# An attention and mixture-of-experts kernel on one core: the second norm's and the router's chained VectorE steps get a tick each

## The chip, the cores and the metric

The kernel runs on one core of one Trainium2 chip. The metric is the device time in microseconds (us) of one execution, the median of three runs. Engines are named PE (TensorE; PEld is its weight load), DVE (VectorE), ACT (ScalarE), POOL (GpSimd) and SP (SyncE, which here only issues DMAs; SPq, POOLq and so on are their queues).

## What is computed

`x` has 8 batches of 512 tokens with 128 channels, all float32.

```
x = x + attention(layernorm(x))          # 16 heads of 8 channels, causal, softmax over 512 keys
x = x + experts(layernorm(x))
# experts: logits = x_n @ Wg (8 experts), the top two of 8 by jax.lax.top_k, gates = softmax of the two logits * alpha
# each token's two experts: layernorm -> fc1 (128 to 512) -> gelu -> fc2 (512 to 128), summed with the gates
```

## The kernel before

**Order of the work.** One list, `schedule`, is built at the start, and every engine walks it and carries out those of its entries that concern it, in that order. The list is ordered by ticks. There are 352 units of attention work, 11 for each of 32 groups of four heads, 44 for each batch; a unit is a bank of scores: one head of 512 columns, one of 384, two of 256 or four of 128. In tick n PE makes the scores of unit n for the row maximum (`pass1`, L644 and L648), then those of unit n-24 again, shifted by the maximum (`pass2`, L665), and, in four of eleven ticks, a row of probabilities times values (`pv`, L680). DVE takes the row maximum of unit n (L940 for one head, L934 for several), ACT the exponential of unit n-24 (L811) and POOL cuts that one's diagonal (L1252). The tables `FRONT`, `APPLY`, `SPLIT`, `FIRST_HALF`, `SECOND_HALF`, `GROUP`, `BACK` and `ROUTE` (L36 to L47) then put all other steps behind the units of given ticks. `FRONT` counts from the start of the batch before, `ROUTE` and `BACK` from the start of their own; since the pattern repeats every 44 ticks, a step at 109 of one batch stands at tick 21 of a period, and this text gives ticks in the period, 0 to 43, in brackets where they matter.

**The score banks.** Both passes share a ring of six banks (`slots`), so PE may begin `pass1` of unit n only when DVE has done the maximum of unit n-3: PE runs at most three ticks ahead of DVE.

**The bank `misc`.** All other PE results go through one bank, in the order maxT [6], xnT [8], q [10], the attention's output projection [13], k [15], maxT [17], zT [24], gate [26], maxT [28], v [31], rank [36], maxT [39]. PE claims it (`claim`) only when the result before it has been read (semaphore `s_free`). A reader (DVE or ACT) takes a result at the start of the next tick, or ahead of the next use of the bank if that stands in the same tick. xnT, q, k, v and zT are read by ACT (L769, L778, L823), the others by DVE.

**First norm of the next batch.** DVE `ln_stats` [1] and `aggregate` [3] (mean and variance, then `var_eps`), POOL `rsqrt` [3] (L1163), DVE `ln_apply` four times [6] (L893), then PE xnT, q and k. POOL's `split` makes the bf16 parts of q and k, SP lays them out by DMA (`stack`).

**The batch's second norm and router.** DVE `r_stats` [14], `r_agg` [17], POOL `rsqrt_two` [17] (L1184), DVE `make_z` [21] (four rows L893 and `ratio` L976), PE zT [24] (L602), gate [26] (L707), ACT `copy_z` [26], DVE `top_two` [30] (L987 to L1005), POOL `second_gate` [31] (L1191), DVE `combine` [34] (L1010 to L1020), PE `rank` [36] (L715 to L721), whose reader on DVE, `put_places` (L1026 to L1034), runs ahead of the maximum of tick 37. POOL then sends the 512 tokens with their two copies off with eight indirect DMAs, `dispatch` (L1235), three ticks apart from [35] on; the first waits for `combine` and `put_places`. Within `top_two`, `combine`, `put_places` and the two `agg` steps, an instruction that reads the one before it waits for its end: `link` lets it raise `s_ln` and makes DVE wait for that count at once. There are 15 such links in a batch.

**The last ticks.** `SOONER` moves the steps of batch 6 forward; what of batch 7 lies behind tick 383 is placed by `LATE` between the expert tiles. Batches 0 to 5 are dispatched by tick 364; the table of the first 17 expert tiles is made in ticks 359 to 363 and loading starts at tick 366. Behind the attention come 39 tiles of expert work (L731 to L756).

## Time and profile before

| | |
|---|---|
| median of 3 runs | 540.84 us (540.76 to 541.0) |
| profiled execution, span | 560.3 us |
| busy: PE, DVE, POOL, ACT | 85%, 67%, 65%, 58% of the span |
| a period of 44 ticks with a router in it, steady | 43.09 us |
| granted TensorE clock there | 1.00 |

The profiled execution has no time of its own beside its span; that is 19.5 us above the median. Times below are microseconds from the start of this span. Busy time of short instructions overlaps: the distance of two starts says what one costs.

### The profile page before, as it was taken

How to read it: one execution, taken by the hardware profiler on the slowest of the kernel's cores; microseconds unless marked ns; L12 is line 12 of the kernel's file. 1: busy time of each engine (PE TensorE's matmuls, PEld its weight loads, DVE VectorE, ACT ScalarE, POOL GpSimd, SP SyncE). 2: the span in 40 equal slices, each digit the busy share in tenths (PEclk: the TensorE clock that was granted, in tenths of full speed). 3: DMA queues.
4: the chain of work that ended last, by engine and by line, in shares of the span. 5: the costliest groups of instructions: out<-in, count | busy, mean ns of one | idle time of the engine just before them, and what ended most of it. 6: DMA issues, size and time to landing. Idle time of an engine off the chain costs nothing.

```text
span 560.3 us, 11807 instructions
## 1 busy us (share of the span) xinstructions
PE 473.9 (85%) x3296; PEld 277.1 (49%) x3296; DVE 373.1 (67%) x1316; ACT 322.9 (58%) x661; POOL 366.1 (65%) x712
## 2 busy tenths in 40 slices
PE   3379999999999998998898988786992999999930
PEld 1134443543443453443444443364981888888920
DVE  4588878889889889889889997741543521222226
ACT  2137786776676776676676666752550555565610
POOL 5956676586986986987887876955556444445520
PEclk9589999999999999999999999897996899999985
DMA  2323133134233234234224212276642685666439
GB/s 62 93 57 105 65 93 109 58 105 118 68 101 117 78 87 129 73 91 130 75 66 130 71 40 79 79 236 213 219 159 86 213 264 180 216 194 187 154 129 328
DMA packets 52726, 70.83 MB, mean 126 GB/s; under 512 B 11063, under 2 KB 38430, under 8 KB 52662
## 3 DMA queue, kind: packets, MB, share of 16 engines
q1 hardware_dynamic: 47478, 59.19, 34.7%
q0 software_dynamic: 4320, 8.53, 4.5%
q10 hardware_dynamic: 864, 2.36, 1.2%
q8 instruction: 27, 0.44, 0.3%
q14 instruction: 37, 0.30, 0.2%
HBM read 36.49 MB, written 20.94 MB: 102 GB/s over the span
## 4 chain that ended last, share of the span: by engine, by line
PE 51%; DVE 17%; issue 8%; POOL 6%; SPq 5%; DMA 4%; another core or an unknown queue 4%; ACT 3%; ACTq 0%; DVEq 0%; POOLq 0%
PE acc_bank L748 10%; PE slots L739 10%; PE slots L648 7%; PE acc_bank L680 7%; PE slots L665 5%; SPq L496 4%; DVE masked L940 3%; PE misc L616 3%; POOL z_dram L1235 2%; DVE z L893 2%; DVE row_max L934 2%; POOL probs L1252 2%; DMA y_in<-y_dram 2%; PE slots L644 2%
## 5 line engine op out<-in xcount | busy, mean ns | idle before, releaser
L811 ACT ACTIVATE probs<-slots 128x512 f32<-128x512 f32 (+1 forms) x352 | 185.6, 562 | 86.0 <-PE slots L665 79.2
L940 DVE CUSTOM_DVE_ANT_0 masked<-slots,causal_row 128x512 bf16<-128x512 f32 (+1 forms) x256 | 148.9, 614 | 20.8 <-PE slots L648 20.7
L648 PE MATMUL slots<-stack_k,stack_q 125*128 125x256 bf16 (+3 forms) x512 | 128.5, 307 | 19.4 <-DVE row_max L940 7.5
L1252 POOL TENSOR_SCALAR_AFFINE_SELECT probs<-probs 128x128 f32<-128x128 f32 (+2 forms) x352 | 116.1, 350 | 41.3 <-ACT probs L811 37.4
L665 PE MATMUL slots<-stack_q,stack_k 128*128 128x256 bf16 (+3 forms) x512 | 125.6, 301 | 2.9 <-DVE row_max L934 1.5
L1282 POOL DMA_INDIRECT y_dram<-y,z_in x71 | 69.7, 982 | 73.4 <-DVE y L1126 56.8
L841 ACT ACTIVATE hidden<-slots,w_in 128x256 f32<-128x256 f32 (+1 forms) x156 | 63.1, 455 | 82.6 <-PE acc_bank L748 29.2
L680 PE MATMUL acc_bank<-probs,v 128*32 128x512 f32 (+3 forms) x1024 | 95.6, 447 | 3.4 <-POOL probs L1252 2.7
L648 PEld LDWEIGHTS slots<-stack_k,stack_q 125*128 125x128 bf16 x512 | 48.3, 99 | 95.4 <-DVE row_max L940 49.7
L1235 POOL DMA_INDIRECT z_dram<-z,pos x64 | 63.6, 994 | 32.1 <-DVE pos L1034 17.7
L748 PE MATMUL acc_bank<-hidden,w_in 128*128 128x256 f32 (+1 forms) x312 | 73.0, 376 | 7.8 <-issue 4.0
L934 DVE TENSOR_REDUCE row_max<-slots 128x2 f32<-128x512 f32 (+1 forms) x96 | 63.7, 689 | 14.0 <-PE slots L648 13.2
L739 PE MATMUL slots<-hdnT,w_in 128*128 128x256 f32 (+1 forms) x312 | 71.1, 372 | 1.4 <-ACT hdnT L834 0.7
L748 PEld LDWEIGHTS acc_bank<-hidden,w_in 128*128 128x128 f32 x312 | 54.6, 196 | 15.9 <-ACT hidden L841 5.8
L739 PEld LDWEIGHTS slots<-hdnT,w_in 128*128 128x128 f32 x312 | 57.4, 197 | 9.8 <-issue 1.9
L665 PEld LDWEIGHTS slots<-stack_q,stack_k 128*128 128x128 bf16 x512 | 46.0, 98 | 25.7 <-issue 6.5
L1126 DVE TENSOR_TENSOR y<-slots,z_in 128x256 f32<-128x256 f32 (+1 forms) x39 | 15.6, 400 | 54.4 <-issue 33.5
L1120 DVE TENSOR_SCALAR yT<-acc_bank,w_in 128x256 f32<-128x256 f32 (+1 forms) x39 | 17.8, 457 | 49.8 <-PE acc_bank L748 37.4
L680 PEld LDWEIGHTS acc_bank<-probs,v 128*32 128x32 f32 x1024 | 20.4, 108 | 36.9 <-issue 17.2
L644 PE MATMUL slots<-causal,ident_b 128*128 128x256 bf16 (+1 forms) x96 | 30.6, 319 | 0.2 <-DVE row_max L940 0.2
L834 ACT ACTIVATE hdnT<-slots,w_in 128x256 f32<-128x256 f32 (+1 forms) x39 | 21.2, 543 | 2.8 <-PE slots L731 2.8
L756 PE MATMUL slots<-ident,yT 128*128 128x128 f32 x71 | 14.6, 280 | 8.0 <-issue 7.6
(168 smaller groups left out, 523.1 us busy)
## 6 DMA issues: line engine op xcount, KB each, us to landing
w_in<-in_wpack SPq DMA_DIRECT2D x39, 516.0 KB
o_dram<-oT SPq DMA_DIRECT2D x32, 256.0 KB, 2.3
stack_k<-parts SPq DMA_DIRECT2D x95, 64.0 KB
stack_q<-parts SPq DMA_DIRECT2D x93, 64.0 KB
z_in<-z_dram SPq DMA_DIRECT2D x32, 132.0 KB
xt<-in_x SPq DMA_DIRECT2D x8, 256.0 KB, 3.7
onT<-o_dram SPq DMA_DIRECT2D x8, 256.0 KB
o_inv<-inv_dram SPq DMA_DIRECT2D x8, 256.0 KB
```

Source lines behind the costliest of these rows:

```text
L648: mm = pe.matmul(cols[:, i, :], q[0:K1, hh, blk * P:blk * P + P], k[0:K1, hh, 0:w], start=len(heads) == 1, stop=True, skip_group_check=True)
L665: mm = pe.matmul(cols[:, i, :], k[0:K2, hh, blk * P:blk * P + P], q[0:K2, hh, blk * P:T], start=True, stop=True)
L680: mm = pe.matmul(acc_bank[32 * h:32 * h + 32, row * P:T], v1[:, b % 2, row, HPG * hg + h, :], p, start=(row == 0), stop=(row == PV_ORDER[- ...
L739: pe.matmul(half(slots[:, k, :], i), weights(i)[:, k * P:k * P + P], hdnT[:, i % 2, 0:rows_of(i)], start=True, stop=True)\
L748: mm = pe.matmul(half(acc_bank[:, :], i), weights(i)[:, F + k * C:F + k * C + C], hidden[:, i % 2, k, 0:rows_of(i)], start=k == 0, stop=k ...
L811: act.activation(probs_of(n), columns(n, slot), ACT.Exp, scale=SCALE).then_inc(s_exp, 1)
L841: act.activation(hidden[:, i % 2, k, 0:rows_of(i)], half(slots[:, k, :], i), ACT.Gelu_apprx_tanh, bias=aux(i, 2 + k))\
L934: dve.tensor_reduce(largest, columns(n, slot), AX.X, ALU.max).then_inc(s_max, 1)
L940: dve.tensor_tensor_reduce(out=masked[:, n % MASKED, 0:w], in0=slots[:, slot, 0:w], in1=causal_row[:, T - w:T], scale=1.0, scalar=NEG, op0 ...
L1235: pool.indirect_dma_start(out=z_dram[:, :], out_offset=bass.IndirectOffsetOnAxis(ap=pos[:, b % 2, i:i + 1], axis=0), in_=z[:, b % 2, j, n, ...
L1252: pool.affine_select(out=diag, in_=diag, compare_op=ALU.is_ge, fill=0.0, base=0, pattern=[[0, len(heads)], [1, P]], channel_multiplier=-1) ...
L1282: pool.indirect_dma_start(out=y_dram[:, :], out_offset=bass.IndirectOffsetOnAxis(ap=z_in[:, i % Z_RING, n, ID:ID + 1].bitcast(U32), axis=0 ...
```

## The change

The steps of the second norm and of the router of batches 0 to 5 are cut up: each instruction (or pair) that another waits for becomes an entry of its own in the tick table. `link` becomes `step` (raise the count) and `stepped` (wait for it, ahead of the next step). The same instructions are issued; the row `base` gets a second copy, so that its update no longer waits for its reader. The new ticks in the period, for batches 0 to 5: stats [14, 15], aggregate [16], variances and POOL's root [17], the four rows of z [23, 24, 25, 26], zT [27], copy [29], gate [30], maximum [31], index [32], difference [33], scaled and POOL's `second_gate` [34], pick [35], select [36], rank [37], sum [38], first gate and mask of places [39], second gate and sum of places [40], alpha and store of places [41], store of gates and the first dispatch [42]. Batch 5's dispatches lie two ticks apart instead of three. Batches 6 and 7 keep their order. The first norm of batches 1 to 7: aggregate [2], variance and POOL's root [3], rows [7, 8, 8, 9], xnT [10], q [12], k [17], and the splits and stacks up to two ticks later. In tick 17, k stands ahead of maxT.

```diff
--- before.py
+++ after.py
@@ -33,21 +33,29 @@
 PV_LAG = 7
 
 
-FRONT = {"ln_stats": 1, "ln_agg": 3, "xnT": 8, "q": 10, "k": 15, "v": 31}
-APPLY = (6, 6, 6, 6)
-SPLIT = ((11, 12, 16, 18), (17, 18, 26, 29))
-FIRST_HALF = ((15, 20, 22), (19, 28, 31))
-SECOND_HALF = ((29, 30, 31), (32, 33, 34))
+FRONT = {"ln_stats": 1, "ln_agg": 2, "ln_var": 3, "xnT": 10, "q": 12, "k": 17, "v": 31}
+APPLY = (7, 8, 8, 9)
+SPLIT = ((13, 14, 18, 20), (19, 20, 28, 31))
+FIRST_HALF = ((17, 22, 24), (21, 30, 33))
+SECOND_HALF = ((29, 30, 31), (34, 35, 36))
 GROUP = {"max_parts": 11, "maxT": 17}
 BACK = {"residual": 40, "o_load": 45, "o_invert": 56, "o_spread": 61, "o_scale": 65,
         "proj": 68}
-ROUTE = (("r_stats", 102), ("r_agg", 105), ("r_root", 105), ("r_z", 109), ("zT", 112), ("gate", 114), ("r_top", 118),
-         ("r_exp", 119), ("r_copy", 114), ("r_comb", 122), ("rank", 124))
-DISPATCH, DISPATCH_STEP = 123, 3
+ROUTE = (("r_stats", 102, 0), ("r_stats", 103, 1), ("r_agg", 104), ("r_var", 105), ("r_root", 105),
+         ("r_z", 111, 0), ("r_z", 112, 1), ("r_z", 113, 2), ("r_z", 114, 3), ("zT", 115), ("gate", 118), ("r_copy", 117),
+         ("r_max", 119), ("r_index", 120), ("r_diff", 121), ("r_scaled", 122), ("r_exp", 122), ("r_pick", 123),
+         ("r_sel", 124), ("rank", 125), ("g_sum", 126), ("g_first", 127), ("g_second", 128), ("p_mask", 127),
+         ("g_alpha", 129), ("p_sum", 128), ("g_store", 130), ("p_store", 129))
+STEPS_OF = {"r_stats": (("r_stats", 0), ("r_stats", 1)), "r_agg": (("r_agg",), ("r_var",)),
+            "r_z": tuple(("r_z", n) for n in range(4)),
+            "r_top": (("r_max",), ("r_index",), ("r_diff",), ("r_scaled",), ("r_pick",), ("r_sel",)),
+            "r_comb": (("g_sum",), ("g_first",), ("g_second",), ("g_alpha",), ("g_store",)),
+            "places": (("p_mask",), ("p_sum",), ("p_store",))}
+LAST_ROUTE = (("r_stats", 94), ("r_agg", 95), ("r_root", 97), ("r_z", 101), ("zT", 109), ("gate", 111), ("r_copy", 111),
+              ("r_top", 115), ("r_exp", 116), ("r_comb", 116), ("rank", 118), ("places", 119))
+DISPATCH, DISPATCH_STEP, LAST_EARLY_STEP = 130, 3, 2
 BY_SCALAR = (("stack", 0, 0, 1, 0), ("stack", 0, 0, 2, 0), ("stack", 0, 1, 2, 0))
-SOONER = {(6, "o_invert"): 8, (6, "o_spread"): 8, (6, "o_scale"): 8, (6, "proj"): 8, (6, "r_stats"): 8,
-          (6, "r_agg"): 10, (6, "r_root"): 8, (6, "r_z"): 8, (6, "zT"): 3, (6, "gate"): 3,
-          (6, "r_top"): 3, (6, "r_exp"): 3, (6, "r_copy"): 3, (6, "r_comb"): 6, (6, "rank"): 6}
+SOONER = {(6, "o_invert"): 8, (6, "o_spread"): 8, (6, "o_scale"): 8, (6, "proj"): 8}
...
     for b in range(B):
         n = NG * UNITS * b
-        for name, m in ROUTE:
-            at(n + m - SOONER.get((b, name), 0), name, b)
+        if b < EARLY_BATCHES:
+            for name, m, *part in ROUTE:
+                at(n + m, name, b, *part)
+        else:
+            for name, m in LAST_ROUTE:
+                for step, *part in STEPS_OF.get(name, ((name,),)):
+                    at(n + m, step, b, *part)
         for i in range(2 * NT):
-            at(n + DISPATCH + DISPATCH_STEP * i - SOONER.get((b, "dispatch"), 0), "dispatch", b, i)
+            step = LAST_EARLY_STEP if b == EARLY_BATCHES - 1 else DISPATCH_STEP
+            at(n + DISPATCH + step * i, "dispatch", b, i)
         if b == EARLY_BATCHES - 1:
             for i, step in enumerate(TABLE):
...
+            def step(ins):
+
+                ins.then_inc(s_ln, 1)
+                chain[0] += 1
+
+            def stepped():
+
+                dve.wait_ge(s_ln, chain[0])
+
...
-            def mean_variance():
+            def mean_variance(*_):
                 dve.wait_ge(s_stats, stats_no[0])
                 for n in range(NT):
                     last = dve.bn_aggr(mean_var[:, n, :], stats[:, n, :])
-                link(last)
-
-            def aggregate(*_):
-                mean_variance()
+                step(last)
+
+            def add_eps(*_):
+                stepped()
                 dve.tensor_scalar(var_eps[:, :], mean_var[:, :, 1], EPS, None, ALU.add).then_inc(s_var, 1)
                 variance_no[0] += 1
 
...
-            def make_z(b):
-                wait(dve, s_rtwo, b + 1)
-                wait(dve, s_disp[b % 2], 16 * 2 * NT * (b // 2))
-                normalise(z[:, b % 2, 0, :, 0:C], xt[:, NT * b:NT * b + NT, :], rstd_two[:, 0, :]).then_inc(s_z, 1)
-                dve.tensor_tensor(ratio[:, :], var_two[:, 0, :], rstd_two[:, 0, :], ALU.mult).then_inc(s_ratio, 1)
+            def make_z(b, n):
+                if n == 0:
+                    wait(dve, s_rtwo, b + 1)
+                    wait(dve, s_disp[b % 2], 16 * 2 * NT * (b // 2))
+                ins = normalise(z[:, b % 2, 0, :, 0:C], xt[:, NT * b:NT * b + NT, :], rstd_two[:, 0, :], (n,))
+                if n == NT - 1:
+                    ins.then_inc(s_z, 1)
...
-            def top_two(b):
+            def find_max(b):
 
                 wait(dve, s_free, misc_no[("gate", b)] + 1)
                 for n in range(NT):
                     last = dve.max(top[:, n, :], gate_in[:, n, :])
-                link(last)
+                step(last)
+
+            def find_index(b):
+                stepped()
                 for n in range(NT):
                     last = dve.max_index(top_at[:, n, :], top[:, n, :], gate_in[:, n, :])
-                link(last)
+                step(last)
+
+            def difference(b):
+                wait(dve, s_second, b)
+                dve.wait_ge(s_ratio, b + 1)
+                stepped()
+                dve.tensor_tensor(denom[:, :], ratio[:, :], rstd_two[:, 1, :], ALU.mult)
+                step(dve.tensor_tensor(diff[:, :], top[:, :, 1], top[:, :, 0], ALU.subtract))
+
...
+            def gate_sum(b):
                 wait(dve, s_second, b + 1)
-                link(dve.tensor_scalar(denom[:, :], second[:, :], 1.0, None, ALU.add))
-                link(dve.reciprocal(gates[:, 0, :], denom[:, :]))
-                link(dve.tensor_tensor(gates[:, 1, :], gates[:, 0, :], second[:, :], ALU.mult))
+                step(dve.tensor_scalar(denom[:, :], second[:, :], 1.0, None, ALU.add))
+
+            def gate_first(b):
+                stepped()
+                step(dve.reciprocal(gates[:, 0, :], denom[:, :]))
+
...
-            def put_places(b):
+            def find_places(b):
                 wait_filled(dve, ("rank", b))
                 if b == 0:
-                    link(dve.tensor_copy(base[:, :], region[:, :]))
-                link(dve.tensor_tensor(place_of[:, :, :], misc[:, 0:NT * E].rearrange("p (n e) -> p n e", e=E),
-                                       base[:, :].rearrange("p (a e) -> p a e", a=1).broadcast_to([P, NT, E]), ALU.add))
-                dve.tensor_tensor(base[:, :], misc[:, NT * E:NT * E + E], base[:, :], ALU.add).then_inc(s_free, 1)
-                link(dve.tensor_tensor(by_place[:, :, :, :].rearrange("p j n e -> p j (n e)"),
+                    link(dve.tensor_copy(base[:, 0, :], region[:, :]))
+                step(dve.tensor_tensor(place_of[:, :, :], misc[:, 0:NT * E].rearrange("p (n e) -> p n e", e=E),
+                                       base[:, b % 2:b % 2 + 1, :].broadcast_to([P, NT, E]), ALU.add))
+                dve.tensor_tensor(base[:, (b + 1) % 2, :], misc[:, NT * E:NT * E + E], base[:, b % 2, :], ALU.add)                   .then_inc(s_free, 1)
+
+            def mask_places(b):
+                stepped()
+                step(dve.tensor_tensor(by_place[:, :, :, :].rearrange("p j n e -> p j (n e)"),
...
```

The other steps (`scaled`, `pick_two`, `select`, `gate_second`, `gate_alpha`, `gate_store`, `sum_places`, `store_places`) are cut out of the old functions in the same way.

## Rows read from the trace of the kernel before

**Rows 1.** The page: busy us, share of the span and instructions.

```profile
PE 473.9 (85%) x3296; PEld 277.1 (49%) x3296; DVE 373.1 (67%) x1316; ACT 322.9 (58%) x661; POOL 366.1 (65%) x712
```

**Rows 2.** Windows: us, busy (count) of PE, PEld, DVE, ACT, POOL, granted clock, DMA.

```profile
60.45:97.37 36.92, 36.13 (x290) 16.03 (x288) 29.44 (x95) 28.16 (x57) 24.34 (x68) 1.00 0.30 90
184.20:227.29 43.09, 39.76 (x322) 18.03 (x316) 38.47 (x142) 30.07 (x59) 34.98 (x76) 1.00 0.33 96
```

**Rows 3.** Waits in 199.17:242.26, one period: us, times, longest us.

```profile
PEld slots L648 <- DVE row_max L940: 6.9, 10, 1.2
...
POOL z_dram L1235 <- DVE pos L1034: 2.5, 1, 2.5
...
PEld acc_bank L680 <- POOL probs L1252: 1.5, 5, 0.4
...
PE misc L602 <- DVE max_rows L948: 1.0, 1, 1.0
...
DVE xn L893 <- POOL rstd L1163: 0.9, 1, 0.9
```

**Rows 4.** Timeline of DVE inside one router: start us, us.

```profile
213.27 0.22 DVE L1015 TENSOR_TENSOR by_alpha<-pick,alpha_s 128x64 f32<-128x64 f32 x1
213.53 0.22 DVE L1018 TENSOR_REDUCE alpha_of<-by_alpha 128x8 f32<-128x64 f32 x1
213.78 0.17 DVE L1019 COPY z<-token_ids 128x8 int32<-128x8 int32 x1
213.86 0.17 DVE L1020 TENSOR_TENSOR z<-alpha_of,gates 128x8 f32<-128x8 f32 x1
```

**Rows 5.** Timelines of DVE and POOL, and DVE's groups by line (busy, mean ns).

```profile
208.72 0.54 DVE L996 TENSOR_TENSOR denom<-ratio,rstd_two 128x4 f32<-128x4 f32 x1
...
207.97 1.27 POOL L1276 TENSOR_TENSOR xt<-xt,bp_s 128x512 f32<-128x512 f32 x1
...
L893 DVE TENSOR_SCALAR z<-xt,mean_var,rstd_two 128x128 f32<-128x128 f32 x32 | 14.9, 525 | 1.2 <-POOL rstd_two L1184 1.2
...
L893 DVE TENSOR_SCALAR xn<-xt,mean_var,rstd 128x128 f32<-128x128 f32 x32 | 9.1, 344 | 5.1 <-POOL rstd L1163 5.1
```

**Rows 6.** Timeline of PE and ACT around results in `misc`.

```profile
235.37 1.13 PE L616 MATMUL misc<-xnT,wqkv_s 128*128 128x512 f32 x2
236.33 0.33 PE L648 MATMUL slots<-stack_k,stack_q 125*128 125x384 bf16 x1
236.53 0.69 ACT L778 ACTIVATE qk<-misc,bqk_s 128x512 f32<-128x512 f32 x1 [0.39 <-PE misc L616]
...
201.03 0.63 PE L602 MATMUL misc<-ident,z 128*128 128x128 f32 x4 [0.22 <-DVE z L893]
...
201.69 0.60 ACT L769 ACTIVATE zT<-misc 128x512 f32<-128x512 f32 x1 [0.25 <-PE misc L602]
```

**Rows 7.** Timeline of POOL behind the router.

```profile
216.43 1.05 POOL L1235 DMA_INDIRECT z_dram<-z,pos  x1 [2.52 <-DVE pos L1034]
...
226.15 1.04 POOL L1163 TENSOR_TENSOR rstd<-var_eps,minus_half 128x4 f32<-128x4 f32 x1
```

**Rows 8.** Timeline of PE: gate, rank, and the unit held up behind it.

```profile
202.83 0.95 PE L707 MATMUL misc<-wg_s,zT 128*128 128x8 f32 x8
203.64 0.32 PE L648 MATMUL slots<-stack_k,stack_q 125*128 125x384 bf16 x1
...
213.19 0.18 PE L715 MATMUL misc<-sel,tri_b 128*128 128x32 bf16 x1
...
213.40 0.32 PE L648 MATMUL slots<-stack_k,stack_q 125*128 125x384 bf16 x1
...
214.69 0.34 PE L648 MATMUL slots<-stack_k,stack_q 125*128 125x384 bf16 x1 [0.75 <-DVE row_max L940]
```

**Rows 9.** Timeline of PE at the attention's end.

```profile
354.23 1.06 PE L680 MATMUL acc_bank<-probs,v 128*32 128x512 f32 x8 [0.89 <-POOL probs L1252]
...
359.28 0.64 PE L680 MATMUL acc_bank<-probs,v 128*32 128x256 f32 x8 [1.80 <-POOL probs L1252]
```

73 lines of the change are left out of this document (45 added, 28 removed).

## The prediction

> **What bounds the kernel now.** I began with the page's busy shares: PE 473.9 of 560.3 us, DVE 373.1, POOL 366.1 [rows 1]. No engine is full on the whole, so the stage has to be looked at. The change moves nothing but steps of the attention, which repeats every 44 ticks; so the next view was the windows of one such period. Two of them are a measurement in themselves: from the rows of the first norm to the next such rows it is 36.92 us where no router runs and 43.09 us where one does [rows 2]. A router thus costs 6.2 us a batch, six times. In its period PE is busy 39.8 us, DVE 38.5, POOL 35.0: three engines at 81 to 92%, none of them full, tied by the ring of six banks. Then the waits of that period [rows 3]: the largest of PE is for a row maximum of DVE, 6.9 us over 10 times; POOL waits once, 2.5 us, for the router's places; PE waits 1.0 us at xnT, and DVE 0.9 us for the first norm's root. The timelines say why. Within a router DVE does eleven small instructions between two maxima, and PE, at most three ticks ahead, runs dry: 0.75 us at 214.69 [rows 8]. In other stretches (228 to 241) PE has hardly a gap. So the pace changes hands, and this decides the sum: a microsecond saved on DVE counts where DVE leads, one added on PE counts where PE leads.
>
> **The parts of the change, for one period.** The number of instructions stays the same; what changes is waiting and place.
>
> *Links.* Of 15 links 12 get a maximum between the two instructions, and the waits are then met when they come up. Three stay: the mask of places stands right behind the first gate, and the sum and the store of places right behind a step of the gates, and each waits for the instruction ahead of it. Price: linked instructions of the router start 0.26 and 0.25 us apart, two without a link 0.08 [rows 4]. The unlinked one is itself 0.05 shorter (0.17 against 0.22), so I take 0.12 a link; the ends are 0 (if a small instruction between two maxima costs more than one in a row) and 0.17. 12 x 0.12 = 1.4 us off DVE, nearly all in the stretch that DVE leads: **-1.4**, ends -2.0 and 0.
>
> The Trainium skill speaks against this term: "VectorE: DVE Perf Modes", section "The DRAIN you can't avoid", says a semaphore behind every instruction costs a chain of copies nothing, and advises to save instructions and not semaphores. By it the term would be 0; the rows above show otherwise.
>
> *The bunch.* Beyond the links, spreading puts 0.1 to 0.6 us behind each maximum in place of 2.4 us behind one, so the ring of three ticks covers it. PE's dry spells behind the router are 0.75 us [rows 8], and much of that is the links again; I take **-0.4**, ends -0.8 and 0.
>
> *First norm's rows.* They come four ticks behind their variance instead of three, and POOL is less behind, so DVE's 0.9 us for the root [rows 3] goes. What is late next is PE's xnT: the last row is at tick 9, xnT at 10, and PE again waits for DVE, as it did for 1.0 us [rows 3]. **-0.3**, ends -0.9 and +0.4.
>
> *Second norm's rows.* A row of z takes 525 ns on average where the same instruction for the first norm takes 344 [rows 5]; `denom` took 0.54 us and ended with a POOL instruction that had started before it (207.97 + 1.27 = 209.24, 208.72 + 0.54 = 209.26) [rows 5]. So DVE is held up by POOL at these. At 23 to 26 the rows stand clear of the two splits in tick 20 in part. Of 4 x 0.18 and some 0.4 of the small ones I take half: **-0.5**, ends -1.0 and 0.
>
> *First dispatch.* POOL arrives at 213.91 and waits 2.52 us [rows 7], diagonals of later units behind it, and is then without a gap until the root at 226.15 [rows 7]. Now places and gates are due at ticks 41 and 42 and the dispatch at 42. POOL arrived about one maximum ahead of DVE, so I expect 0.7 us of wait. PE waited for cuts 1.5 us in this period [rows 3]: **-0.6**, ends -1.5 and 0.
>
> *The bank `misc`.* This is the cost side; each new neighbour makes PE wait for a reader. (a) k and maxT share tick 17: PE could go on at 236.33, ACT has read k by 236.53 + 0.6 = 237.1 [rows 6]; +0.8. (b) q at 12, projection at 13: the same read, less the 0.45 us of tick 13's matmuls; +0.35. Both lie in the stretch that PE leads: **+1.15**. (c) zT 27, maxT 28: ACT's copy begins 0.25 behind the transposes' last (201.69) and takes 0.6 [rows 6], less 0.3 of matmuls; +0.45. (d) gate 30, v 31: v waits until DVE, up to three ticks behind, has read the gate; PE is dry for the bank, then DVE for the 0.8 to 0.9 us of v; +0.5, ends 0 and 1.0. Both lie where DVE leads, and I count half: **+0.5**. (e) select 36, rank 37: PE waits for DVE, but DVE has the maximum of 37 (0.6 us) to do meanwhile, and a rank takes 0.21 [rows 8]: 0, with an upper end of +0.7.
>
> *The queues.* SP issues the same DMAs, the last stack two ticks later (36 in place of 34), eight ticks before the next batch's first unit, so 0. POOL's `second_gate` waits for DVE's scaled difference of its own tick, cover: the sum that uses it is four ticks later, so 0; without the cover it would be a POOL instruction of 1 us on DVE's path.
>
> *Sum.* -1.4 - 0.4 - 0.3 - 0.5 - 0.6 + 1.15 + 0.5 = -1.55 us a period; times 6, -9.3. In periods without a router only the first norm's changes count, and there PE leads (36.13 of 36.92 busy [rows 2]): +0.8 for k and +0.35 for q less 0.3, about +0.9 once. At the end of the attention PE waits for POOL's cuts (0.89 and 1.80 us [rows 9]); batch 5's dispatches, packed into ticks 350 to 364, are seven instead of five behind tick 352, but POOL has not lost its 2.5 us ahead of them: 0, ends -1 and +2. Batches 6 and 7 and the expert tiles keep their order: 0. Total -8.4.
>
> The sum is made on the profiled execution: 560.3 to 551.9 us. That one is 19.5 us longer than the median of 540.84; the attention is not where such time would go by anything the trace shows, so I carry the difference over unscaled: 540.84 - 8.4 = **532.5 us**.
>
> **The rivals.**
>
> *A. PE alone sets the pace.* If spreading hides all of the router's DVE work, a period is the one without router plus PE's own work for it: 36.92 + gate 0.81 + rank 0.21 [rows 8] + projection, like the gate, 0.85 + zT 0.4 + 0.8 for k = 40.0 us. That is 3.1 x 6 = 18.6 less, and 0.9 more for the front: **523 us**. For it: DVE was 29.4 of 36.92 busy without a router [rows 2], so there is room. Against it: the router adds 9.0 us to DVE and 10.6 to POOL. Chance 0.15.
>
> *B. Slower: the bank `misc`.* If DVE's savings fall where PE leads or is held by `misc`, what remains is the links (-1.4) against all of the bank's waits (0.8 + 0.35 + 0.45 + 0.5): +0.7 a period, 4.2 in six, and +0.9 for the front: 5 us, **546 us**. It decides from the point where PE's new waits pass DVE's savings, 2.1 against 1.4. For it: 228 to 241 is PE's; k, q and xnT are in it. Against it: PE's 6.9 us of waits for maxima show DVE leading elsewhere. Chance 0.20.
>
> *C. No change.* If the links are free, since a small instruction by itself between two large ones costs about what it did, the sum is -0.15 a period, 0.9 in six, against +0.9 for the front: **541 us**. This would also be the time if POOL set the pace. Chance 0.10.
>
> The DRAIN rule of the Trainium skill's "VectorE: DVE Perf Modes" is this case; the unlinked start 0.08 us behind speaks against it.
>
> **How the numbers follow.** The forecast has 0.55, A 0.15, B 0.20, C 0.10. A measurement of this kernel can tell 0.2%, 1.1 us, from no change. Faster 0.70, same 0.10, slower 0.20. The range leaves out the outer half of A (0.07) and of B (0.10): 523 to 546 us.
>
> **What the changed profile would show.** Links: between two maxima one or two small DVE instructions, none 0.25 behind another but the three named. Bunch: the wait of PE for L940 below 5 us a period. POOL's wait ahead of its first dispatch below 1 us. First norm: DVE's wait for the root gone, PE's wait at xnT still there. Bank: gaps of 0.8 us on PE between k and maxT and 0.3 to 0.5 at the projection and at the maxT behind zT. A period of 41.5 us instead of 43.09. The prediction is wrong if the period stays above 42.8 or falls under 40.3, or if the expert part changes by over 2 us.

## The result, and the profile of the changed kernel

The changed kernel is slower: 557.43 us (median of four runs) against 540.92 for the kernel before on the same chip, ratio 1.030 [1.028, 1.032]. The prediction said 532.5.

The two profiled executions can't be compared as wholes. In that of the kernel before (560.3 us) ACT stood idle for 23.4 us in the expert part, for something the trace calls "remote"; in that of the changed kernel (554.1 us) it did not. On one of the chips used below the kernel before takes 541 us again, and the four traces taken there (e9 to e12) show no such waits; on the others it takes 562 to 565 us, and every trace taken there shows 12 to 25 us of them for ACT in the expert part. From batch 2 on the attention of the changed kernel has none, and its periods repeated within 0.05 us on another chip (e5).

So the attention is measured by a landmark that both kernels have 352 times, once in each tick: the start of DVE's row maximum. From that of tick 5 to that of tick 5 of the next batch it takes, in us:

| batch | 0 | 1 | 2 | 3 | 4 | 5 | 6 | last maximum at |
|---|---|---|---|---|---|---|---|---|
| before | 32.98 | 36.92 | 42.27 | 43.62 | 43.10 | 43.08 | 41.63 | 345.0 |
| changed | 33.42 | 39.28 | 44.77 | 45.56 | 45.38 | 45.37 | 44.25 | 358.7 |

A period is 2.28 us longer instead of 1.55 shorter, and batch 1, which has no router in it yet, is 2.36 longer. The last maximum comes 13.7 us later. What follows it is longer too: 217.7 us in e5 against 215.3 in the kernel before, both with "remote" waits, and 1.5 of these 2.4 us lie ahead of PE's last product with v, where the prediction had 0. The windows of batch 4, cut at the maxima of the ticks 5, 12, 19, 24, 27, 31, 37, 43 and 5, show where (us, then busy us and count of PE, PEld, DVE, ACT, POOL, the granted clock, DMA share, GB/s). First the kernel before:

```profile
182.31:189.06 6.75, 5.67 (x52) 3.09 (x55) 5.87 (x20) 4.24 (x9) 6.16 (x13) 1.00 0.29 101
189.06:196.65 7.59, 7.59 (x52) 3.02 (x51) 6.11 (x29) 6.05 (x12) 6.86 (x16) 1.00 0.19 55
196.65:202.30 5.65, 5.26 (x44) 2.48 (x43) 5.39 (x11) 4.13 (x8) 5.42 (x12) 1.00 0.37 110
202.30:204.10 1.80, 1.80 (x13) 1.21 (x12) 1.80 (x9) 1.63 (x4) 1.61 (x5) 1.00 0.57 159
204.10:210.02 5.92, 5.92 (x56) 3.17 (x55) 4.53 (x27) 4.32 (x10) 4.02 (x8) 1.00 0.20 51
210.02:216.08 6.06, 4.65 (x39) 1.57 (x39) 5.79 (x23) 3.58 (x7) 3.19 (x9) 1.00 0.41 123
216.08:219.88 3.80, 3.71 (x37) 1.80 (x36) 3.49 (x13) 1.98 (x5) 3.24 (x7) 1.00 0.55 138
219.88:225.41 5.53, 5.13 (x37) 1.68 (x34) 5.50 (x23) 4.11 (x8) 4.50 (x12) 1.00 0.31 97
```

The same stretches of the changed kernel:

```profile
188.65:195.13 6.48, 5.40 (x55) 2.99 (x56) 5.86 (x20) 3.87 (x8) 6.06 (x13) 1.00 0.37 114
195.13:204.81 9.68, 8.56 (x53) 3.29 (x47) 6.33 (x29) 6.11 (x12) 8.72 (x17) 1.00 0.15 45
204.81:209.91 5.10, 4.92 (x41) 2.34 (x41) 4.84 (x9) 4.31 (x10) 4.57 (x8) 1.00 0.42 123
209.91:212.54 2.63, 1.34 (x10) 0.27 (x10) 2.63 (x12) 1.27 (x3) 2.33 (x8) 1.00 0.42 117
212.54:217.48 4.94, 4.52 (x42) 2.73 (x42) 2.79 (x10) 2.89 (x6) 2.89 (x8) 1.00 0.13 34
217.48:223.23 5.75, 4.91 (x37) 2.67 (x37) 5.18 (x28) 4.68 (x9) 4.37 (x10) 1.00 0.43 133
223.23:229.00 5.77, 5.49 (x56) 2.55 (x57) 5.00 (x25) 2.90 (x6) 2.56 (x9) 1.00 0.41 113
229.00:234.03 5.03, 4.33 (x33) 1.28 (x31) 5.03 (x24) 3.79 (x8) 3.70 (x10) 1.00 0.27 86
sum 45.38, PE 39.47 PEld 18.10 DVE 37.65 ACT 29.81 POOL 35.20; mean PE 4.93 PEld 2.26 DVE 4.71 ACT 3.73 POOL 4.40
```

Neither of the two hot engines has more to do in the sum: DVE 37.65 us against 38.47, PE 39.47 against 39.73 (with 327 records for 330, so PE's difference may be one of recording). Yet PE stands idle for 5.9 us instead of 3.4. The largest loss is in the second row: before, PE was full there (7.59 of 7.59); now the same seven ticks take 9.68, of which PE works 8.56. The ticks 37 to 43 lose nearly as much (5.77 for 3.80), but the ten ticks ahead of them gain 1.3 (10.69 for 11.98). In the rows from 209.91 to 217.48 the two engines take turns: DVE 2.63 of 2.63 with PE at 1.34, then PE 4.52 of 4.94 with DVE at 2.79. The ring holds three ticks and does not bridge that.

The waits of one period of the changed kernel (190.91 to 236.29; us, times, longest), which answer to [rows 3]:

```profile
PEld slots L663 <- DVE row_max L964: 6.8, 8, 1.3
...
DVE masked L964 <- PE slots L663: 2.5, 3, 1.5
POOL z_dram L1300 <- issue: 2.4, 8, 0.8
DVE row_max L958 <- PE slots L663: 2.2, 5, 0.6
...
PE misc L617 <- DVE xn L917: 1.0, 1, 1.0
DVE xt L988 <- PE misc L710: 1.0, 1, 1.0
PE misc L730 <- DVE sel L1047: 1.0, 1, 1.0
...
DVE gate_in L1007 <- PE misc L722: 0.8, 1, 0.8
PE misc L702 <- ACT qk L793: 0.8, 1, 0.8
...
DVE xn L917 <- POOL rstd L1228: 0.6, 1, 0.6
```

POOL's 2.5 us for the places are gone. What is new stands beside `misc` and on DVE: rank waits for select, the gate's copy for the gate, the maxima's transpose for ACT's reading of k. PE's wait for the maxima is what it was, 6.8 against 6.9. In the timeline of PE and ACT (start, us, in brackets the idle time ahead):

```profile
197.14 0.69 ACT L793 ACTIVATE qk<-misc,bqk_s 128x512 f32<-128x512 f32 x1 [1.36 <-PE misc L631]
197.88 1.16 PE L710 MATMUL misc<-wp_s,onT 128*128 128x128 f32 x8 [0.34 <-ACT qk L793]
...
203.10 0.24 PE L702 MATMUL misc<-ident_b,max_parts 128*48 128x128 bf16 x1 [0.78 <-ACT qk L793]
...
223.45 0.18 PE L730 MATMUL misc<-sel,tri_b 128*128 128x32 bf16 x1 [1.01 <-DVE sel L1047]
```

The two waits for ACT that the prediction priced at 0.35 and 0.8 are there with 0.34 and 0.78. And DVE beside POOL at the first of z's rows:

```profile
207.61 1.17 POOL L1309 TENSOR_TENSOR parts<-qk,parts 128x512 bf16<-128x512 f32 x1
208.19 1.79 DVE L917 TENSOR_SCALAR z<-xt,mean_var,rstd_two 128x128 f32<-128x128 f32 x1
208.73 1.16 POOL L1309 TENSOR_TENSOR qk<-qk,parts 128x512 f32<-128x512 f32 x1
210.51 0.34 DVE L917 TENSOR_SCALAR z<-xt,mean_var,rstd_two 128x128 f32<-128x128 f32 x1
```

A row takes 0.34 us by itself; the one that began inside POOL's split took 1.79 and ended 0.09 behind the second split. The splits had moved two ticks with the first norm's part, and so had followed the rows that were moved away from them.

### The profile page after: what moved, and what is told of

It reads as the page before. It is cut to its first block, busy times and chain, and to the rows that moved or that the text cites. A ratio compares the mean times of both kernels' runs of the same rounds, so it can differ in the third digit from the quotient of the medians.

```text
span 554.1 us, 11776 instructions
## 1 busy us (share of the span) xinstructions
PE 467.1 (84%) x3264; PEld 274.2 (49%) x3296; DVE 366.4 (66%) x1316; ACT 321.2 (58%) x661; POOL 369.0 (67%) x712
## 3 DMA queue, kind: packets, MB, share of 16 engines
q10 hardware_dynamic: 864, 2.36, 1.2%
## 4 chain that ended last, share of the span: by engine, by line
PE 54%; DVE 16%; issue 11%; POOL 6%; DMA 5%; SPq 3%; ACT 3%; ACTq 0%; DVEq 0%; POOLq 0%
PE slots L754 11%; PE acc_bank L763 10%; PE acc_bank L695 8%; PE slots L663 7%; PE slots L680 5%; DVE masked L964 4%; DVE row_max L958 3%; PE misc L631 3%; SPq L511 2%; POOL probs L1317 2%; DMA y_in<-y_dram 2%; PE misc L617 2%; POOL z_dram L1300 2%; DVE xn L917 2%; ACT qk L793 2%
## 5 line engine op out<-in xcount | busy, mean ns | idle before, releaser
L826 ACT ACTIVATE probs<-slots 128x512 f32<-128x512 f32 (+1 forms) x352 | 182.4, 562 | 92.3 <-PE slots L680 83.2
L964 DVE CUSTOM_DVE_ANT_0 masked<-slots,causal_row 128x512 bf16<-128x512 f32 (+1 forms) x256 | 152.3, 614 | 26.9 <-PE slots L663 25.9
L1317 POOL TENSOR_SCALAR_AFFINE_SELECT probs<-probs 128x128 f32<-128x128 f32 (+2 forms) x352 | 119.0, 352 | 66.1 <-ACT probs L826 61.5
L680 PE MATMUL slots<-stack_q,stack_k 128*128 128x384 bf16 (+3 forms) x507 | 124.4, 301 | 2.9 <-DMA stack_q<-max_rows 2.5
L763 PE MATMUL acc_bank<-hidden,w_in 128*128 128x256 f32 (+1 forms) x312 | 68.1, 361 | 0.0
L754 PEld LDWEIGHTS slots<-hdnT,w_in 128*128 128x128 f32 x312 | 56.2, 193 | 9.1 <-issue 1.9
L680 PEld LDWEIGHTS slots<-stack_q,stack_k 128*128 128x128 bf16 x512 | 45.8, 98 | 28.8 <-issue 8.3
L763 PEld LDWEIGHTS acc_bank<-hidden,w_in 128*128 128x128 f32 x312 | 53.0, 190 | 5.0
L1188 DVE TENSOR_TENSOR y<-slots,z_in 128x256 f32<-128x256 f32 (+1 forms) x39 | 15.6, 400 | 45.8 <-PE slots L771 45.8
L964 DVE DVE_READ_ACCUMULATOR2_ANT row_max<- 128x1 f32 x256 | 21.0, 82 | 0.0
L659 PE MATMUL slots<-causal,ident_b 128*128 128x256 bf16 (+1 forms) x69 | 20.3, 294 | 0.4 <-DVE row_max L964 0.2
```

What stands on the lines that cost most here:

```text
L680: mm = pe.matmul(cols[:, i, :], k[0:K2, hh, blk * P:blk * P + P], q[0:K2, hh, blk * P:T], start=True, stop=True)
L754: pe.matmul(half(slots[:, k, :], i), weights(i)[:, k * P:k * P + P], hdnT[:, i % 2, 0:rows_of(i)], start=True, stop=True)\
L763: mm = pe.matmul(half(acc_bank[:, :], i), weights(i)[:, F + k * C:F + k * C + C], hidden[:, i % 2, k, 0:rows_of(i)], start=k == 0, stop=k ...
L826: act.activation(probs_of(n), columns(n, slot), ACT.Exp, scale=SCALE).then_inc(s_exp, 1)
L964: dve.tensor_tensor_reduce(out=masked[:, n % MASKED, 0:w], in0=slots[:, slot, 0:w], in1=causal_row[:, T - w:T], scale=1.0, scalar=NEG, op0 ...
L1317: pool.affine_select(out=diag, in_=diag, compare_op=ALU.is_ge, fill=0.0, base=0, pattern=[[0, len(heads)], [1, P]], channel_multiplier=-1) ...
```

## The experiments

All of them keep the changed kernel's code and move steps among ticks; the diffs of the tables are shortened to the entries that change. The table gives stretches of one period, measured as above and taken from batches in which the granted clock was 1.00 (batch 4, or the batch named), then the periods of batches 3, 4 and 5 as they came, and the ratio to the kernel before on the same chip. e12 has no row, since the clock fell in each of its batches from 3 on.

| run | 5-12 | 12-19 | 19-27 | 27-37 | 37-43 | 43-5 | periods | ratio |
|---|---|---|---|---|---|---|---|---|
| before | 6.75 | 7.59 | 7.45 | 11.98 | 3.80 | 5.53 | 43.6 43.1 43.1 | |
| changed | 6.48 | 9.68 | 7.73 | 10.69 | 5.77 | 5.03 | 45.6 45.4 45.4 | 1.030, e5 1.028 |
| e1 | 7.61 | 7.58 | 7.46 | 11.21 | 4.32 | 5.24 | 43.8 43.4 43.4 | 1.008 [1.005, 1.012] |
| e2 | 7.10 | 9.68 | 8.05 | 11.83 | 4.33 | 5.03 | 49.4 46.0 46.0 | 1.036 [1.032, 1.039] |
| e3 | 7.92 | 7.59 | 6.77 | 12.08 | 4.13 | 5.23 | 45.4 43.7 43.8 | 1.009 [1.007, 1.011] |
| e4 (batch 3) | 7.26 | 7.59 | 8.67 | 9.59 | 5.77 | 5.23 | 44.1 46.8 45.3 | 1.017 [1.010, 1.024] |
| e6 | 7.11 | 9.07 | 8.04 | 11.84 | 4.33 | 5.03 | 45.8 45.4 45.4 | 1.026 [1.019, 1.032] |
| e7 | 6.04 | 7.59 | 8.64 | 9.60 | 5.51 | 5.31 | 45.7 42.7 45.7 | 1.005 [1.000, 1.009] |
| e8 | 6.93 | 7.58 | 8.67 | 11.22 | 4.32 | 5.24 | 44.3 44.0 46.7 | 1.015 [1.008, 1.022] |
| e9 | 6.48 | 9.68 | 7.72 | 10.33 | 5.77 | 5.03 | 45.2 45.0 45.0 | 1.029 [1.028, 1.031] |
| e10 (batch 6) | 7.76 | 7.68 | 8.77 | 10.69 | 5.77 | | 52.6 49.8 51.3 | 1.052 [1.049, 1.054] |
| e11 (batch 5) | 6.69 | 7.69 | 8.07 | 10.42 | 5.52 | 5.29 | 43.9 44.8 43.7 | 1.015 [1.013, 1.018] |
| e13 | 6.25 | 9.67 | 6.86 | 11.16 | 5.80 | 5.03 | 44.4 44.8 44.7 | 1.024 [1.020, 1.029] |
| e14 (batch 5) | 6.40 | 7.59 | 7.54 | 10.03 | 7.11 | 5.35 | 44.8 45.4 44.0 | 1.017 [1.013, 1.021] |
| e15 (batch 3) | 5.89 | 7.58 | 7.55 | 9.60 | 5.55 | 5.30 | 41.5 42.0 41.5 | 1.005 [1.003, 1.008] |
| e16 | 5.98 | 9.76 | 6.86 | 10.68 | 5.99 | 5.12 | 44.2 44.4 44.6 | 1.036 [1.033, 1.039] |
| e17 | 5.96 | 7.58 | 7.59 | 9.59 | 5.58 | 5.30 | 41.5 41.6 42.6 | 0.999 [0.997, 1.001] |
| e18 | 5.99 | 7.58 | 7.59 | 9.58 | 5.37 | 5.51 | 42.4 41.6 42.3 | 0.995 [0.993, 0.997] |

### The three parts alone (e1 to e4)

**e1**: all steps back at their old ticks; only the steps of the places come one maximum later.

```diff
-FRONT = {"ln_stats": 1, "ln_agg": 2, "ln_var": 3, "xnT": 10, "q": 12, "k": 17, "v": 31}
-APPLY = (7, 8, 8, 9)
...
-DISPATCH, DISPATCH_STEP, LAST_EARLY_STEP = 130, 3, 2
+FRONT = {"ln_stats": 1, "ln_agg": 3, "ln_var": 3, "xnT": 8, "q": 10, "k": 15, "v": 31}
+APPLY = (6, 6, 6, 6)
...
+         ("r_z", 109, 0), ("r_z", 109, 1), ("r_z", 109, 2), ("r_z", 109, 3), ("zT", 112), ("gate", 114), ("r_copy", 114),
...
+DISPATCH, DISPATCH_STEP, LAST_EARLY_STEP = 123, 3, 3
```

> The changed code with every step put back to its old tick (cut-up steps of one group share a tick, so each waits for the one ahead of it as under the old links; the steps behind the place of a token run one maximum later than before). Theory (ticks decide, the code that cuts them up costs nothing): within 0.5% of the kernel before, 538 to 543.5 us. Rival (more entries and semaphore counts cost by themselves): 545 us or more.

Period 43.42, ratio 1.008: the rewritten code, with the places one maximum later, costs 0.3 us a period. That is a sum of larger differences, +0.86 at ticks 5 to 12 and -0.77 at 27 to 37 among them. The base for the parts is 43.42.

**e2**: e1 with the changed first norm, splits and stacks.

```diff
-FRONT = {"ln_stats": 1, "ln_agg": 3, "ln_var": 3, "xnT": 8, "q": 10, "k": 15, "v": 31}
-APPLY = (6, 6, 6, 6)
-SPLIT = ((11, 12, 16, 18), (17, 18, 26, 29))
...
+FRONT = {"ln_stats": 1, "ln_agg": 2, "ln_var": 3, "xnT": 10, "q": 12, "k": 17, "v": 31}
+APPLY = (7, 8, 8, 9)
+SPLIT = ((13, 14, 18, 20), (19, 20, 28, 31))
...
```

> Old ticks, but the first norm's rows, xnT, q, k, splits and stacks at their new ticks. Theory of the bank (k's read by ACT ahead of maxT in tick 17, 0.78 us, and q's ahead of the projection, 0.34 us, lie in a stretch that PE leads; both were measured as waits of PE in the changed kernel): plus 1.1 us in each of seven periods, 549 us (545 to 552). Rival of the prediction's sum (the root's 0.9 us on DVE comes off against it): 541 to 543 us.

46.01: +2.6 us a period, more than twice the forecast's cost, though nothing of the router moved. The stretch 12 to 19 has 2.1 of it (9.68 against 7.58); 19 to 37 loses 1.2 more, and 37 to 12 gives 0.7 back. In batch 3 (49.4) the granted clock fell to 0.85 at ticks 5 to 12.

**e3**: e1 with the changed second norm, the bunches one tick later.

```diff
-         ("r_z", 109, 0), ("r_z", 109, 1), ("r_z", 109, 2), ("r_z", 109, 3), ("zT", 112), ("gate", 114), ("r_copy", 114),
+         ("r_z", 111, 0), ("r_z", 112, 1), ("r_z", 113, 2), ("r_z", 114, 3), ("zT", 115), ("gate", 118), ("r_copy", 117),
```

> Old ticks, but the second norm's rows at ticks 23 to 26, zT 27, copy 29, gate 30, and the router's chains kept in bunches, one tick later than before (31, 35, rank 37, places 38, dispatch from 36). Theory of the bank and the port (the first row waits for POOL's splits, 1.8 us; zT waits for the last row 0.6; maxT for zT's read 0.4; v for the gate's read): plus 1 to 2 us in six periods, 547 to 553 us. Rival (these lie where DVE leads and are hidden): 541 us.

43.70: +0.3. The rows gain what was hoped (19 to 27: 6.77 against 7.46), and the later gate takes it back (27 to 37: 12.08 against 11.21): DVE's copy, ahead of its maximum, waits 0.8 us for PE's gate. In batch 3 (45.4) the clock fell to 0.82 at ticks 5 to 12.

**e4**: e1 with the router's steps and dispatches at the changed ticks.

```diff
+         ("r_max", 119), ("r_index", 120), ("r_diff", 121), ("r_scaled", 122), ("r_exp", 122), ("r_pick", 123),
+         ("r_sel", 124), ("rank", 125), ("g_sum", 126), ("g_first", 127), ("g_second", 128), ("p_mask", 127),
+         ("g_alpha", 129), ("p_sum", 128), ("g_store", 130), ("p_store", 129))
```

> First norm and rows of the second at their old ticks (rows in tick 21, zT 24, gate 26), but the router's steps a tick each from 31 to 42, rank one tick behind the selection, dispatch from 42. Theory (the spread itself saves DVE the links and POOL its 2.5 us, and rank costs PE 1.0 us of which half counts): 1 to 1.5 us less in six periods, 532 to 536 us. Rival (the spread is what costs, because PE waits at rank and the steps between maxima delay each of them): 544 us or more.

Not faster but slower, though the stretch 27 to 37 falls by 1.6 us (9.59). It is lost at 37 to 43 (+1.45), at 19 to 27 (+1.2), and to the clock: in batches 4, 5 and 6 PE's granted clock fell below 1.00 at ticks 24 to 31 (0.52 at the least). In batch 3, where it stayed, the period is 44.1 against e1's 43.8, so the router's part by itself costs 0.3 us, and the rest of the 1.9 us that batch 5 shows over e1 is the clock. The parts alone, with the clock held, make 2.6 + 0.3 + 0.3 = 3.2, together 2.0 over e1: they are not additive.

### Which pair in `misc` (e5, e6, e7, e9, e10, e11)

**e5**: the changed kernel again, on the chip of e1 to e4.

> The changed kernel, edited in nothing, beside the others on their chip. Its period was 45.38 us; the four runs so far gave 43.42 with the old ticks, 46.01 with the first norm's part alone, 43.70 with the second norm's part alone and 45.31 with the router's part alone. The period of the attention should repeat within 0.1, and the ratio to the kernel before lie at 1.03, as it did. If the ratio were under 1.015 here, the slowdown would hang on the chip and not on the order of steps.

Periods 45.55, 45.35, 45.34 and ratio 1.028 [1.021, 1.034]: nothing of the slowdown hangs on the chip.

**e6**: e2 with k two ticks earlier.

```diff
-"xnT": 10, "q": 12, "k": 17
+"xnT": 10, "q": 12, "k": 15
```

> The run with the first norm's part alone (period 46.01, 583.7 us beside 564.6 for the kernel before), with k back at tick 15, so that it no longer shares tick 17 with the transpose of the maxima; rows, xnT, q, splits and stacks stay late. Theory, that each pair of neighbours in the bank misc costs the stretch it lies in: the ticks from 17 to 19 took 1.0 us more there than in the kernel before, so the period comes to 45.0 and the time to 577.5. Rival, that the later rows and splits cost and not the neighbours: period 45.8 or more, 582 or more.

45.42. The stretch 12 to 19 falls by 0.61, from 9.68 to 9.07: the price of k beside the maxima's transpose. 1.5 us are left.

**e7**: e4 with rank and places two ticks later.

```diff
-("rank", 125), ("p_mask", 127), ("p_sum", 128), ("p_store", 129), DISPATCH 130
+("rank", 127), ("p_mask", 129), ("p_sum", 130), ("p_store", 131), DISPATCH 132
```

> The run with the router's steps a tick each (period 45.31, 574.2 us), with rank and the steps of the places two ticks later, so that PE does not come to rank while DVE is still at select; the dispatches start two ticks later too. Theory: PE's 1.0 us of waiting at rank takes away its lead, and the ticks behind it, 38 to 42, cost 2 us more than before because PE and DVE then wait for each other in turn; with rank two ticks behind select the period falls to 44.2 or less and the time to 568 or less. Rival: the spreading itself costs, since every small instruction between two maxima holds up the ring there: period 45.1 to 45.4, 573 to 575 us.

Where the clock stayed, 42.68, the first period below that of the kernel before; 37 to 43 is only 0.26 better than in e4 (5.51), most came at ticks 5 to 12 (6.04 against 6.93 in e4's batch 4), where DVE waits 0.2 us for POOL's root instead of 1.0; the dispatches, two ticks later, are part of this run. In batches 3 and 5 the clock fell. The windows of ticks 27 to 31 in batch 4 and, from tick 19 on, in batch 5:

```profile
206.54:210.43 3.89, 3.89 (x39) 1.61 (x39) 2.41 (x9) 2.52 (x6) 3.67 (x11) 1.00 0.14 38
```

```profile
240.57:247.41 6.84, 5.22 (x43) 2.48 (x43) 6.57 (x13) 4.06 (x8) 6.56 (x10) 1.00 0.53 153
247.41:249.59 2.18, 2.18 (x13) 1.55 (x12) 1.96 (x9) 2.09 (x5) 1.93 (x5) 0.72 0.15 50
249.59:256.08 6.49, 6.49 (x39) 1.88 (x39) 2.60 (x9) 2.24 (x5) 4.51 (x11) 0.57 0.17 44
```

The same 39 matmuls take 3.89 us at 1.00 and 6.49 at 0.57. Ahead of it PE worked 5.22 of 6.84 us, with one wait of 1.5 us for z's rows; batches 4 and 6 had the same ahead and kept their clock.

**e9**: the changed kernel with v two ticks later.

```diff
-"k": 17, "v": 31
+"k": 17, "v": 33
```

> The changed kernel (period 45.38 and 45.35 us, ratio 1.0275 on this chip) with v at tick 33 in place of 31, so that no projection waits in misc for DVE's reading of the gate at tick 30. Theory: the stretch from tick 30 to 31 takes 1.85 us there and 0.96 in the runs whose gate is at 26, so 0.9 us a period come back: 44.5, ratio 1.018. Rival, that the loss only moves to the next tick in which PE must wait: 45.2 or more.

Only 0.37 us. The tick that was to shrink, 30 to 31, stayed at 1.86 us; the one behind it shrank. So it is not v waiting for the gate but DVE waiting for it, as in e3.

**e10**: the changed kernel with the projections apart.

```diff
-"xnT": 10, "q": 12, "k": 17, APPLY = (7, 8, 8, 9)
+"xnT": 9, "q": 11, "k": 15, APPLY = (6, 7, 7, 8)
```

> The changed kernel with q a tick earlier and k two, so that q no longer stands in the tick before the output projection and k not in that of the maxima's transpose; xnT and the rows go one tick earlier with them; splits and stacks stay late. Theory: these two pairs cost 1.5 us (ticks 12 to 14) and 0.6 to 0.7 (17 to 19): period 43.2, ratio 1.004. Rival, that it is the late splits, stacks and rows: 45 or more.

The stretch 12 to 19 does what the theory said: 7.68, PE full. And the kernel is the second slowest of all. The rows of the first norm, a tick earlier, meet POOL's root: DVE waits 1.2 us for it and PE 1.6 us for the rows, so ticks 5 to 12 take 7.76 instead of 6.48. z's rows meet the splits (19 to 27: 8.77), and in batches 3 to 5 the clock is 0.50 behind them:

```profile
208.75:214.88 6.13, 4.98 (x42) 2.34 (x41) 5.87 (x8) 4.98 (x11) 5.92 (x9) 1.00 0.44 138
214.88:217.52 2.64, 1.34 (x10) 0.27 (x10) 2.64 (x12) 0.60 (x1) 2.34 (x8) 0.95 0.31 83
217.52:225.58 8.06, 7.95 (x41) 4.47 (x42) 2.79 (x11) 3.10 (x6) 2.93 (x8) 0.50 0.16 43
```

In batch 6 the same ticks took 4.94 us at 1.00, with as much work of PE ahead.

**e11**: e10, with the two other pairs apart too (rank, places and dispatches as in e7).

```diff
-"v": 31, ("rank", 125), DISPATCH 130
+"v": 33, ("rank", 127), DISPATCH 132
```

> The changed kernel with all four pairs apart: q 11 and k 15 as in the run before, v 33, rank with the places two ticks later and the dispatches with them. If the prices add up (1.5 + 0.6 + 0.9 + 0.5 = 3.5 us a period), the period is 41.9 and the ratio 0.98; if they hide each other, as the sum of the three parts alone (2.6 + 0.3 + 1.9 = 4.8 against 2.0 measured for all) suggests, 43 or more. A drop of the granted clock in single batches, as the three runs with late dispatches had, would show as batches 3 us longer than the rest.

43.7 to 43.9 where the clock stayed: all pairs apart bring 1.7 us of the hoped 3.5. The ticks 5 to 19, which took 14.34 us before and 16.16 in the change, are back at 14.38, so with q and k moved back nothing of the loss there is left. It stays 0.6 above the kernel before, at 19 to 27 and at the gate.

### Where POOL's dispatches stand (e8, e12 to e18)

**e8**: e1 with the later dispatches.

```diff
-DISPATCH, DISPATCH_STEP, LAST_EARLY_STEP = 123, 3, 3
+DISPATCH, DISPATCH_STEP, LAST_EARLY_STEP = 130, 3, 2
```

> The run with the changed code at the old ticks (period 43.42, 569.3 us), with the dispatches from tick 42 in place of 35, as in the change; nothing else moved. POOL then has its places long before it comes to the first dispatch, so its wait of 2.8 us goes. The prediction took -0.6 us a period for this: 42.8, 565.5 us. Theory now, that POOL's wait is slack, since the kernels that lost it have POOL waiting for ACT's exponentials instead (6.3 us against 2.5): period 43.3 to 43.5, 569 us. Rival, that the dispatches collide with the root and the next batch's first units: 44.0 or more, 573 us or more.

The prediction's -0.6 is refuted: +0.5, and a fall of the clock in batches 5 and 6. The part that it had in mind is there: without POOL's wait for the places DVE waits 1.0 us for the first norm's root instead of 1.7, and ticks 5 to 12 fall by 0.7. But 19 to 27 takes 1.2 us more, because POOL, with a dispatch at ticks 16 and 19, splits while z's rows run.

**e12**: e7 with denser dispatches.

```diff
-DISPATCH, DISPATCH_STEP, LAST_EARLY_STEP = 132, 3, 2
+DISPATCH, DISPATCH_STEP, LAST_EARLY_STEP = 132, 2, 2
```

> Old front and second norm, the router's steps a tick each with rank two ticks late, and the dispatches two ticks apart in place of three, so that the last is at tick 14 and none stands among the splits of ticks 16 to 18. In the run with three ticks between them the tick of z's rows took 4.06 us instead of 2.87, since POOL's splits ran beside the rows, and in the batches 3 and 5 the granted clock fell to half behind it (45.65 against 42.68 us). Theory: without the collision the rows take 2.9 us, the clock stays, and the period is 41.5 in every batch, 558 us beside 564.7 for the kernel before. Rival, that the dense dispatches make PE wait for POOL's cuts: 42.5 or more.

The theory was the wrong way round: 48.5 to 49.8 us, ratio 1.061 [1.059, 1.063], the slowest. A denser queue makes POOL later still at its splits:

```profile
204.43 4.28 DVE L917 TENSOR_SCALAR z<-xt,mean_var,rstd_two 128x128 f32<-128x128 f32 x4 [0.88 <-POOL rstd_two L1249]
204.64 1.14 POOL L1309 TENSOR_TENSOR parts<-qk,parts 128x512 bf16<-128x512 f32 x1
205.75 1.14 POOL L1309 TENSOR_TENSOR qk<-qk,parts 128x512 f32<-128x512 f32 x1
```

Four rows take 4.28 us, and the clock falls in every batch from 3 on.

**e13**: the changed kernel with the dispatches of batches 0 to 4 from 156 on.

```diff
-            at(n + DISPATCH + step * i, "dispatch", b, i)
+            late_start = 26 if b < EARLY_BATCHES - 1 else 0
+            at(n + DISPATCH + late_start + step * i, "dispatch", b, i)
```

> The changed kernel with the dispatches of batches 0 to 4 from tick 24 of the next batch on (156, 159, ... in place of 130, 133, ...), so that in the ticks 42 to 19 POOL has the splits and cuts alone; nothing else moved. Theory, that the dispatches among the splits make these late and let them run beside z's rows: the first row of z, 1.79 us, takes 0.5 or less, the ticks 19 to 24, 5.10 us, take 4.0, and the period goes from 45.38 to 44.2, ratio 1.02. Rival, that the dispatches' place is slack as POOL's wait was: 45.3 and 1.03. If the second root or the router's second gate now stands behind a dispatch (1.0 us), the ticks 30 to 37 grow instead.

The stretch 19 to 27 falls by 0.87 to 6.86, what e3 had: the second norm's part does gain 0.6 once POOL is in time. The third case came too: 27 to 37 grows by 0.5.

**e14**: e7 with the same dispatches (132 + 24).

```diff
+            late_start = 24 if b < EARLY_BATCHES - 1 else 0
```

> Old front and second norm, the router's steps a tick each with rank two ticks behind select (in the run of that order, 42.68 us in a period whose clock stayed and 45.65 in one where it fell), with the dispatches from tick 24 of the next batch on in place of 44. Theory: the ticks 19 to 24 took 6.84 us there and 5.66 before, since z's rows ran beside POOL's splits, and the granted clock fell only behind that; with POOL's splits in time the period is 41.5 in every batch and the kernel beats both others, ratio 0.985. Rival, that the dispatches then collide with the splits of ticks 26 and 29 and the second norm's root: 42.7 or more.

19 to 27 as foreseen (7.54), no fall of the clock there, but a new loss at 37 to 43 (in batches 3 and 4 with the clock at 0.80). In batch 5:

```profile
259.44 1.01 POOL L1301 DMA_INDIRECT z_dram<-z,pos  x1 [0.58 <-POOL max_parts L1333]
...
261.07 1.05 POOL L1257 TENSOR_TENSOR second<-euler,diff 128x4 f32<-128x4 f32 x1
...
262.15 0.26 DVE L1052 TENSOR_SCALAR denom<-second 128x4 f32<-128x4 f32 x1 [1.42 <-POOL second L1257]
...
263.07 0.19 PE L731 MATMUL misc<-sel,tri_b 128*128 128x32 bf16 x1 [2.15 <-DVE max_rows L973]
```

The dispatch delays the second gate, DVE stands for it, and PE for DVE.

**e15**: e7 with batches 0 to 3 from 167 on, tick 35 of the next batch.

```diff
+            late_start = 35 if b < EARLY_BATCHES - 2 else 0
```

> As e14, but batches 0 to 3 dispatch from tick 167 on, which is tick 35 of the next batch: the ticks at which the kernel before dispatches, one batch later, with the places long known. In e14 the ticks 19 to 24 took 5.74 as foreseen, but 37 to 43 took 7.1 and 8.3 instead of 5.51, since the router's second gate on POOL stood behind the dispatch of tick 33. Theory: first dispatch behind the second gate, last at tick 12, so 5.9 (ticks 5 to 12), 7.6, 5.7, 1.8, 3.9, 5.7, 5.5 and 5.3 (43 to 5): a period of 41.4 without a drop of the clock, 7 us off the attention, ratio 0.99. Rival, that dispatches beside the gates' small steps make PE wait for cuts there: 42.5 or more.

Periods 41.47, 41.97, 41.54 without a fall of the clock. All is lost again in batch 7, where batches 3 and 4 dispatch at once: ticks 12 to 24 take 16.9 us against 11.2 before, and the last maximum is at 344.9, where it was. The profiled execution is one of the faster (562.5 us; the twelve go from 561.4 to 571.8).

**e16**: the changed kernel with these dispatches (130 + 37).

```diff
+            late_start = 37 if b < EARLY_BATCHES - 2 else 0
```

> The changed kernel with the same dispatches as e15 (batches 0 to 3 from tick 167 on); nothing else moved. The ticks 19 to 24 should take 4.2 as in e13 (5.10 in the changed kernel), and 31 to 37 no longer the 6.2 of e13 but 5.75: period 44.4. What is then left over the kernel before, 1.3 us, is the neighbours in misc: 2.1 in the ticks 12 to 19 against what the router saves. Rival, that the dispatches' shift cost nothing: 45.3.

44.2 to 44.6: 1.0 of the 2.28 us is the dispatches' place. The whole is not faster but slower (1.036), as in e15 for its end: ticks 12 to 19 of batch 7 take 10.50 us, 6.24 in the changed kernel.

**e17**: e15 with batch 4 from 147 on.

```diff
+            late_start = (35, 35, 35, 35, 15, 0)[min(b, 5)]
```

> As e15, but batch 4 dispatches from tick 147 of its own count (323, 326, ... 344) in place of 132 (308 to 329), so that it no longer stands among the dispatches of batch 3 (299 to 320). In e15 the periods were 41.5 to 42.0 us as foreseen, but in the last stretches of the attention, where both batches dispatch, the ticks 12 to 24 of batch 7 took 16.9 us instead of 11.2 and the granted clock fell to 0.8, which gave 6 us back. Theory: without that the last maximum starts at 339 us instead of 345.0, and the time is 5 us or 1% below the kernel before, ratio 0.99. Rival, that the end of the attention waits for POOL in any case (batch 5's dispatches follow at once): ratio 1.00.

Last maximum at 342.7, no difference in time that is clear of the noise. The last router has e14's chain again (PE 3.85 us at rank).

**e18**: e17 with the gates two ticks later and rank one earlier.

```diff
-("rank", 127), ("g_sum", 126), ("g_first", 127), ("g_second", 128), ("g_alpha", 129), ("g_store", 130)
+("rank", 126), ("g_sum", 128), ("g_first", 129), ("g_second", 130), ("g_alpha", 131), ("g_store", 132)
```

> As e17, with the sum for the gates and the four steps behind it two ticks later (tick 40 in place of 38), and rank with the places one earlier (tick 38), so that rank no longer shares tick 39 with the transpose of the maxima. In e17 DVE stood 1.43 us at that sum for POOL's second gate in batch 7, and PE 3.85 us at rank for DVE's copy of the maxima's transpose behind it; the ticks 37 to 43 took 10.2 us there against 4.04 before. Theory: they take 5.5 to 6.5 in batch 7, the periods stay at 41.5, the last maximum starts near 339 us and the ratio is 0.99. Rival, that what follows the last maximum (24.7 us to the last product with v in e17, 22.0 before), POOL's dispatches of batch 5, takes the gain back: ratio 0.995 to 1.00.

559.74 against 562.67 us, ratio 0.9946 [0.9926, 0.9966]: 0.5% faster than the kernel before, small but clear of the noise, and so faster than the changed kernel, which was 3% slower. The last maximum is at 340.8; in batch 7 the ticks 37 to 43 still take 7.93 us at a clock of 0.78, not the 5.5 to 6.5 expected.

## Why the prediction was wrong

The sum said -1.55 us a period, the measurement +2.28. Two steps of it failed most: the one on q, which mis-sized a term, and the one on the first dispatch, which had even the sign wrong.

**q.** The step read "q at 12, projection at 13: the same read, less the 0.45 us", +0.35, and priced only the wait in the bank. That wait is 0.34, as said. But q is also 1.13 us of PE's own work [rows 6], and it moved from ticks 5 to 12, where DVE sets the pace (PE busy 5.67 of 6.75), into 12 to 19, where PE was full. There it lengthens the stretch by itself; the ticks it left did not get shorter: with the dispatches at the same ticks they take 5.98 us in e16, with q at 12, and 5.96 in e17, with q at 10. With e6's 0.61 for k the 2.09 us of this stretch are accounted for: 0.61, and 1.48 that e6 leaves, beside 1.13 + 0.34 = 1.47 for q's work and wait; e10 and e11, with q back at 11, are at 7.68 and 7.69. That q's part divides into work and wait in this way is read from the rows; no run separates the two. Batch 1, without a router, pays too: 2.36 us, where the prediction had 0.9, and 1.8 of it in this stretch.

**k and maxT**: +0.8 predicted, wait 0.78, price 0.61. Right.

**Links and bunch** (-1.8 together): DVE's work did fall, to 37.09 us a period in e18 against 38.47 before. But e1, with every step at its old tick, is already at 37.79, so about 0.7 of the 1.38 is the spreading; it is not z's rows, which meet POOL's splits in both (the first takes 1.32 us in e18, the second 1.20 before). A small step alone between two maxima costs less than a linked one: the maximum behind this one starts 0.16 us after it, where linked steps start 0.25 apart [rows 4].

```profile
210.27 0.23 DVE L1040 TENSOR_TENSOR pick<-expert_ids,top_atf 128x64 f32<-128x64 f32 x1
210.43 0.68 DVE L965 CUSTOM_DVE_ANT_0 masked<-slots,causal_row 128x512 bf16<-128x512 f32 x1
```

In time the spread router gave 15.78 - 15.11 = 0.7 us (ticks 27 to 43, before against e7): 2.4 at 27 to 37, and 1.7 lost at 37 to 43, where the small steps of gates and places went. Against e1, which has the same code, it is 0.4 us. The ticks 37 to 43 had had PE 3.71 of 3.80 busy; "nearly all in the stretch that DVE leads" was wrong for where the steps landed. Rival C, free links, is refuted by these rows and by DVE's busy time. The Trainium skill's rule ("VectorE: DVE Perf Modes", section "The DRAIN you can't avoid") that a semaphore behind each instruction costs nothing does not hold for these.

**Second norm's rows** (-0.5): -0.7 in e3, but +0.3 in the change. The step took the rows "clear of the two splits in tick 20 in part" and forgot that the first norm's part moves those splits too. e13 shows the size: -0.87 once POOL is in time. The Trainium skill ("SBUF — State Buffer", section "SBUF: two separate sides") says that GpSimd and those VectorE instructions that use a pair of ports shared with it exclude each other for whole instructions. The 1.79 us beside 0.34 agree with that, if a row is such an instruction, which no run here shows.

**First dispatch** (-0.6): the wait of 2.5 us went, and the period grew by 0.5 (e8), by 1.0 in the change (e16). With a miss of 1.1 to 1.6 us this is the largest. The gain that the step named was real: ticks 5 to 12 fall by 0.7 in e8. It counted only the wait that goes, and not that the dispatches, seven ticks later, now stand among POOL's splits: +1.2 at 19 to 27. With the dispatches at the ticks of the kernel before and no wait for places (e17) ticks 5 to 12 are at 5.96 against 6.75 before, and 19 to 27 at 7.59 against 7.45. The rest of POOL's 2.8 us in e1 was slack: in e8 it waits 5.4 us for ACT's exponentials instead of 2.5. (Nor was POOL "without a gap until the root" in the kernel before: it stood idle for 0.58 us ahead of its dispatch at 224.01.) What costs is which of POOL's steps stands behind a dispatch when another engine comes for it.

**Bank `misc`, the router's side** (+0.5): gate and v were priced as PE waiting for DVE; it is DVE that waits 0.8 us for PE's gate. e3's 27 to 37 is 0.87 over e1's, the changed kernel's 1.1 over e7's; 0.4 of it is v behind the gate (e9). The gate's own 0.8 us of PE work moved into this stretch too, and no run separates it from the wait. Rank behind select, "0, since DVE has the maximum of 37 meanwhile": PE waited 1.01, and moving it away brought 0.26 in its stretch.

**First norm's rows** (-0.3): ticks 5 to 12 are 0.27 shorter, but that the number fits is luck. The dispatches alone take 0.7 off the same stretch (e8), and with them at the same ticks the new rows bring nothing (5.98 in e16 against 5.96 in e17). DVE's wait for the root, which was to go, is still 0.6 us of 0.9. PE waits 1.0 at xnT, as foreseen.

Rival B had the sign and the kind of cause, PE's waits against DVE's savings, but at 0.7 a period; it, too, missed q's work and the dispatches. The longer period holds in every batch, so the time is 16.5 us above where it was and 25 above the forecast. Of the period's 2.28 us, the runs place 2.1 at q and k, 1.0 at the dispatches, 1.1 at the gate and 0.3 at rank, which leaves -2.2 for POOL's wait, the spread router and z's rows. The parts overlap, as e11's 1.7 for an expected 3.5 shows, and the runs don't split them further.

## What to carry to other kernels

When engines are tied by a short ring, a step moved between ticks carries its own duration with it: ask of both stretches, the one left and the one entered, which engine is full there, and count the step's work where its engine is full even if no instruction was added. A wait that an in-order engine loses is worth something only if another engine was waiting behind it, and a step that several others meet at a fixed place (a split beside rows, a gate behind a dispatch) has to be followed through every queue that the change shifts. Cut the period at a landmark that both kernels share and compare the stretches: that showed in one view what the sums by engine hid.

## What the runs showed of the chip

- **PE's clock is in the schedule.** In the kernel before and in the changed one the granted clock is 1.00 (2.4 GHz) from batch 1 on; in most of the runs it fell towards 0.50 (1.2 GHz) in single batches, at a price of 1 to 7 us each, mostly behind a stretch in which DVE held PE up with z's rows (5.22 of 6.84 us busy). The Trainium skill ("TensorE: Matmul & The Clock Gate", section "HAM oscillation — how this bites in real kernels") describes a kernel that goes back to the low clock again and again, for waits that are longer than the work between them. The falls here agree in that they came behind waits, but the longest wait ahead of those in e7 is 1.5 us beside 5.2 us of work. And e7's batch 4 had the same 5.2 of 6.84 ahead and kept its clock, e8's batch 4 too: what decides between them stays open.
- **The places of instructions repeat to 0.05 us, whole executions don't.** The changed kernel's periods were 45.38 and 45.35 us on two chips, while its profiled executions took 554.1 and 576.1 us: the last maximum starts at 358.7 and 358.4, and the difference lies behind it (195.4 and 217.7 us). What the waits for "remote" are stays open.
